# Cross-attention in another order: value projections spread over both pairs of heads, queries projected earlier, and the first batch's own work started on its own

## The chip, the core and the metric

The kernel runs on one core of a Trainium2 chip. The metric is the device time of one execution in microseconds (us). The engines are named as in the profile: PE is TensorE's matrix multiplication and PEld its weight loads, DVE is VectorE, ACT is ScalarE, POOL is GpSimd, SP is SyncE, which here only issues transfers.

## The reference, cut to what matters

Three layers follow one another on x of 4 batches x 256 tokens x 256. The change is in the first alone.

```
x = x + xattn(layernorm(x), ctx, Wq1, Wk1, Wv1, Wk2, Wv2, Wo, bo)   # the layer the change is in
x = x + mixer(layernorm(x), ...)                                    # top-k attention and a scan
x = x + experts(layernorm(x), ...)                                  # 8 experts, 2 of them per token

# xattn: 8 heads of 64, 256 queries, 256 own keys and 4096 context keys in each batch
q = x1 @ Wq1
k = concat(x1 @ Wk1, ctx @ Wk2)
v = concat(x1 @ Wv1, ctx @ Wv2)
attn = softmax(q @ k.T / 8)
return (attn @ v) @ Wo + bo
```

## The kernel before

`cross_attention` works through 16 pairs of heads, `u = 0..15`, four pairs for each of four batches. A pair has 4352 keys, in 17 tiles of 256 (`HG`), and is done in nine steps, `d = 0..8`; a step takes score tiles 2d and 2d+1, the last step only tile 16.

The projections keep single precision by splitting each operand in a high and a low part (`_hi`, `_lo`) and adding three products (`product3`, L609): ACT stores the high part, POOL or DVE subtracts to get the low part. For weights and context it is POOL that subtracts (L342, L347, L353).

While pair u is being scored and weighed, the same steps prepare pair v = u+1: `project_keys(v, d+1)`, 6 matmuls of 512 columns, and `score_for_max` (L677), two rough score products a step whose row maxima DVE reduces (L496). At the end of the pair `turn_maxima` (L688) turns the row maxima for the softmax shift, `store_neg_max` negates them on DVE, and only then can the next pair's `score` begin.

Values are projected for two pairs at a time (c = pair couple), 17 tiles of 12 matmuls each (`project_values`), in the PSUM banks M that `score_for_max` uses too. So a value tile waits until DVE has reduced the latest maxima (`max_reduced`), and the next `score_for_max` waits until ACT has stored the value tile (`v_stored`, L413). `v_due(u, d)` says which tiles belong to a step: before, two tiles in each of steps 2 to 8 of an odd pair, and the last three in steps 0 and 1 of the even pair after it.

The order on each engine is the order in which its function is written; engines meet only at semaphores. PE's order inside a step, before: maxima of the last key group, score tiles, maxima of this one, keys, values (L609), then the tiles of the step before weighed by the values (`weigh`, L722). At the end of a pair PE does the two last maxima products, three `weigh`, `turn_maxima`, then `project_queries(v)` and `project_keys(v, 0)` for the pair after.

DVE in a step: two maxima (L496), two additions of 128x1024 probabilities (L517), one low part of keys (L488). In step 1 it also inverts the sums and normalizes (L522, L531), which releases PE's first `weigh` of the pair.

At a change of batch the next batch's context chunks are loaded, copied and split in steps 3 and on of pair 4k+2 (`chunk_due`), and ACT and DVE split the own tokens (L459, L477) in its step 4. Before the first pair, all eight token tiles are normalized (DVE L104 to L123), turned by PE (L599) and copied (L472), and pair 0's keys, values and maxima are made; this is called the prologue here. Its first DVE instruction waits for x, bo and Wo together (`x_loaded`, 48).

## Time and profile before

| | us |
|---|---|
| median of three runs | 1687.1 (1685.04 to 1692.69) |
| the profiled execution | 1682.5 |
| its span in the trace | 1680.8 |
| prologue, to the first score of pair 0 | 79.7 |
| pairs 0 to 15, to the start of the mixer | about 1110 |
| PE busy over the whole span | 1475.6 (88%) |

The page's slices show PE at nine tenths or more almost all through the first 1180 us; only the first slice and the part after it are lower. Pair starts below are the start of the pair's first `score` matmul (L704). All numbers are of one profiled execution.

Four views are read below. A group of the page holds line, engine, operation and shapes, count, busy us and mean ns, and the idle time before it with its releaser. A row of the waits holds who waited for whom, total us, times and longest us. A row of busy times by stretch holds the stretch and its length in us, then the busy us (and instructions) of PE, PEld, DVE, ACT and POOL, then the clock granted to TensorE as a share of its full speed, the share of DMA time and GB/s. A row of the timeline holds start and duration in us, engine, line, operation, tiles, shape, how many alike were merged (x16) and, in brackets, how long the engine stood idle before it and who released it. The ends of matmuls are modelled, so distances between starts are used here for PE.

### The profile page before, as it was taken

To read this page: it belongs to the slowest core of one execution; us is meant where nothing else is said; L and a number is where in the kernel's file an instruction comes from. 1 tells how busy PE (TensorE), PEld (TensorE's weight loads), DVE (VectorE), ACT (ScalarE), POOL (GpSimd) and SP (SyncE) were. 2 spreads that over 40 slices of the span, in tenths; PEclk is the share of its full clock that TensorE was granted. 3 is DMA by queue.
4 is the path that set the end of the run, shared out by engine and by line. 5 is a ranking of instruction groups with operands and counts; after the bars stand their busy time and mean duration, and the time that the engine had idled before them with its cause. 6 is when DMAs were issued, how large, how long until landed. Compare 5 with 4: busy or idle time off the path is not lost. (4 is left out here: it accounts for less than half of the span.)

```text
span 1680.8 us, 29549 instructions
## 1 busy us (share of the span) xinstructions
PE 1475.6 (88%) x11988; PEld 1130.3 (67%) x11988; DVE 1128.8 (67%) x1287; ACT 711.3 (42%) x954; POOL 448.6 (27%) x270
## 2 busy tenths in 40 slices
PE   5999999999999999999999999999497787826996
PEld 4777776776776677677667777777264444526996
DVE  4587578557657855865876586486586899654663
ACT  3444344434434433343444344344336333223773
POOL 4300024000002400000230010000122999533885
PEclk9999999999999999999999999999799999967998
DMA  5000021000002100000210000000203900092333
GB/s 172 13 11 11 1 86 48 1 14 11 11 14 73 48 1 14 13 9 14 86 35 1 14 20 1 2 1 2 83 1 137 276 1 0 1 324 93 58 63 59
DMA packets 62371, 76.50 MB, mean 46 GB/s; under 512 B 6368, under 2 KB 47968, under 8 KB 61840
## 3 DMA queue, kind: packets, MB, share of 16 engines
q1 hardware_dynamic: 57152, 68.51, 13.3%
q0 software_dynamic: 5088, 6.11, 2.5%
q8 instruction: 99, 1.62, 0.4%
q14 instruction: 32, 0.26, 0.1%
HBM read 58.39 MB, written 17.25 MB: 45 GB/s over the span
## 5 line engine op out<-in xcount | busy, mean ns | idle before, releaser
L496 DVE TENSOR_REDUCE xa_maxes<-psum 128x2 f32<-128x1024 f32 (+1 forms) x288 | 332.5, 1161 | 268.9 <-PE psum L677 268.9
L422 ACT ACTIVATE xa_probs<-psum 128x1024 f32<-128x1024 f32 x272 | 269.1, 1026 | 325.4 <-PE psum L710 312.5
L517 DVE TENSOR_TENSOR xa_prob_sum<-xa_prob_sum,xa_probs 128x1024 f32<-128x1024 f32 x240 | 308.8, 1287 | 11.2 <-ACT xa_probs L422 10.4
L722 PE MATMUL psum<-xa_probs,xa_vals 128*64 128x256 f32 x2176 | 263.1, 385 | 2.2 <-DVE xa_heads_T L531 1.6
L722 PEld LDWEIGHTS psum<-xa_probs,xa_vals 128*64 128x64 f32 x2176 | 146.5, 136 | 92.7 <-issue 23.6
L347 POOL TENSOR_TENSOR xa_w_lo<-xa_stage,xa_w_hi 128x768 fp32r<-128x768 f32 x16 | 31.9, 1994 | 615.4 <-ACT xa_w_hi L382 615.4
L609 PE MATMUL psum<-xa_wv_hi,xa_ctx_hi 128*128 128x256 f32 x512 | 148.3, 290 | 21.2 <-DVE xa_maxes L496 18.4
L704 PE MATMUL psum<-xa_q_hi,xa_k_hi 64*128 64x256 f32 x1088 | 157.2, 285 | 0.6 <-issue 0.6
L708 PE MATMUL psum<-xa_q_hi,xa_k_lo 64*128 64x256 f32 x1088 | 155.1, 281 | 0.0
L710 PE MATMUL psum<-xa_neg_max,xa_ones 64*128 64x256 f32 x1088 | 154.7, 280 | 0.0
L706 PE MATMUL psum<-xa_q_lo,xa_k_hi 64*128 64x256 f32 x1088 | 154.5, 280 | 0.0
L413 ACT ACTIVATE xa_vals<-psum 128x512 f32<-128x512 f32 x136 | 81.2, 597 | 151.6 <-PE psum L609 151.6
L609 PE MATMUL psum<-xa_wv_lo,xa_ctx_hi 128*128 128x256 f32 x512 | 144.7, 283 | 0.0
L609 PE MATMUL psum<-xa_wv_hi,xa_ctx_lo 128*128 128x256 f32 x512 | 144.4, 282 | 0.0
L677 PE MATMUL psum<-xa_k_hi,xa_q_hi 64*128 64x512 f32 (+1 forms) x604 | 124.0, 425 | 16.8 <-issue 14.1
L404 ACT ACTIVATE xa_k_hi<-psum 128x512 fp32r<-128x512 f32 (+1 forms) x151 | 83.1, 555 | 129.6 <-PE psum L609 129.6
L609 PEld LDWEIGHTS psum<-xa_wv_hi,xa_ctx_hi 128*128 128x128 f32 x512 | 97.6, 191 | 41.3 <-issue 40.7
L488 DVE TENSOR_TENSOR xa_k_lo<-psum,xa_k_hi 128x512 fp32r<-128x512 f32 (+1 forms) x151 | 94.6, 630 | 37.9 <-ACT xa_k_hi L404 36.2
L609 PE MATMUL psum<-xa_ctx_hi,xa_w_hi 128*128 128x512 f32 x256 | 115.1, 450 | 2.5 <-issue 2.5
L1699 DVE TENSOR_TENSOR_SCAN mx_drive<-psum,mx_drive 128x768 f32<-128x768 f32 x64 | 110.0, 1743 | 7.7 <-POOL mx_drive L1224 6.9
L1224 POOL TENSOR_TENSOR mx_drive<-mx_xi,mx_rows 128x768 f32<-128x768 f32 x62 | 110.8, 1820 | 0.1
L342 POOL TENSOR_TENSOR xa_ctx_lo<-xa_ctx_in,xa_ctx_hi 128x1024 fp32r<-128x1024 f32 x32 | 84.8, 2652 | 93.8 <-ACT xa_ctx_hi L395 93.8
(319 smaller groups left out, 3013.1 us busy)
## 6 DMA issues: line engine op xcount, KB each, us to landing
xa_ctx_in<-in_ctxT_dram SPq DMA_DIRECT2D x32, 512.0 KB, 3.7
ex_slots<-mx_blank_tile SPq DMA_DIRECT2D x2, 4372.5 KB, 37.1
xa_stage<-in_L_xattn_Wk_dram SPq DMA_DIRECT2D x32, 128.0 KB, 2.4
xa_stage<-in_L_xattn_Wv_dram SPq DMA_DIRECT2D x16, 256.0 KB, 2.9
ex_raw<-in_L_ffn_w_gate_dram SPq DMA_DIRECT2D x8, 512.0 KB, 10.5
ex_raw<-in_L_ffn_w_up_dram SPq DMA_DIRECT2D x8, 512.0 KB, 10.9
ex_raw<-in_L_ffn_w_down_dram SPq DMA_DIRECT2D x8, 512.0 KB, 12.1
ex_xt<-ex_slots SPq DMA_DIRECT2D x15, 265.0 KB, 2.8
```

Of the source, the lines that this page charges most:

```text
L422: nc.scalar.activation(probs[:, n % RING, :], S[:, 2 * (n % 2):2 * (n % 2) + 2, :].rearrange("p h q -> p (h q)"), ACT.Exp, scale=HD ** -0. ...
L496: dve.tensor_reduce(maxes[:, qt, :, g:g + 1], max_banks(v, g, qt)[:, :, 0:group_keys(g)[1]], AX_X, ALU.max).then_inc(max_reduced, 1)
L517: dve.tensor_tensor(prob_sum[:, :], prob_sum[:, :], probs[:, n % RING, :], ALU.add).then_inc(summed, 1)
L609: i = pe.matmul(out, l, r, start=(c == 0 and k == 0), stop=(c == n - 1 and k == 2))
L677: i = pe.matmul(max_banks(v, g, qt)[:, h, part * N1:(part + slots) * N1], q_hi[half[h], v % 2, qt * P:(qt + 1) * P], k_hi[half[h], at:at + ...
L704: pe.matmul(out[h], k[h], q[h], start=True, stop=False)
L706: pe.matmul(out[h], k[h], q[2 + h], start=False, stop=False)
L708: pe.matmul(out[h], k[2 + h], q[h], start=False, stop=False)
L710: i = pe.matmul(out[h], ones[half[h], :], neg_max[half[h], :], start=False, stop=True)
L722: i = pe.matmul(O[half[h], 0:N1], vals[:, 2 * j + t, lanes:lanes + HD], probs[:, n % RING, (2 * h + t) * N1:(2 * h + t + 1) * N1], start=( ...
L1224: pool.tensor_tensor(drive[n % RINGS][:, :], dx[:, ct, :], b_rows[:, s, :], ALU.mult).then_inc(drive_done, 1)
L1699: dve.tensor_tensor_scan(drive[n % RINGS][:, :], decay[n % DECAYS], drive[n % RINGS][:, :], 0.0, ALU.mult, ALU.add).then_inc(scanned, 1)
```

## The change

It has four parts, all in `cross_attention`.

**Values.** `v_due` gives tiles 0 to 4 to steps 3 to 7 of the odd pair, 5 and 6 to its step 8, then 7 and 8, 9 and 10 to steps 0 and 1 of the even pair, and 11 to 16 to its steps 2 to 7. Within a step the value tile stands between the two `weigh`; in step 0 the sums of the pair before (`sum_probs`) go ahead of the values. In step 8 the maxima products are interleaved with the three `weigh`.

**Queries.** `project_queries(u + 2)` moves to the end of pair u, ahead of `turn_maxima`; for that the query and own-key weights are split apart from the context-key weights (`split_query_weights`, ACT and POOL, in step 6), and weights are loaded from step 0 on.

**Batches.** The own tokens stay as normalized rows (`xl_next`) and are turned by PE for one batch at a time (`turn_own`, 4 transposes, in step 0 of pair 4k+2), in the place of 16 transposes in the prologue. Context chunks are split four steps later: chunks 0 and 1 in steps 7 and 8 of pair 4k+2, chunks 2 to 7 in steps 0 to 5 of pair 4k+3.

**Start.** x is loaded in two parts. The first batch (`x_loaded`) is normalized and turned at once. The rest, bo and Wo are loaded between and behind the context chunks (`rest_loaded`, 48), and DVE waits for all three before it normalizes the other six tiles.

```diff
         def v_due(u, d):
             if u % 2 == 1 and u + 1 < U:
-                return [((u + 1) // 2, j) for j in (2 * d - 4, 2 * d - 3) if 0 <= j]
+                return [((u + 1) // 2, j) for j in ((5, 6) if d == STEPS - 1 else (d - 3,)) if j >= 0]
             if u % 2 == 0 and u > 0:
-                return [(u // 2, j) for j in (2 * d + 14, 2 * d + 15) if j < HG]
+                return [(u // 2, j) for j in ((7, 8) if d == 0 else (9, 10) if d == 1 else (9 + d,)) if j < HG]
             return []
...
-            at = (u % PAIRS - 2) * STEPS + d - 3
+            at = (u % PAIRS - 2) * STEPS + d - 7
...
-            sp.dma_start(X1[:, :, :], x.rearrange("b (t p) d -> p (b t) d", p=P)).then_inc(x_loaded, 16)
-            sp.dma_start(bo_sb, bo.rearrange("(a d) -> a d", a=1).broadcast_to([P, D])).then_inc(x_loaded, 16)
-            sp.dma_start(wo_sb[:, :, :], wo.rearrange("(c p) n -> p c n", p=P)).then_inc(x_loaded, 16)
+            sp.dma_start(X1[:, 0:QT, :], x[0, :, :].rearrange("(t p) d -> p t d", p=P)).then_inc(x_loaded, 16)
...
             load_pair(0)
-            for c in range(CHUNKS):
+            load_chunk(0, 0)
+            load_values(0)
+            load_chunk(0, 1)
+            sp.dma_start(X1[:, QT:TT, :], x[1:B, :, :].rearrange("b (t p) d -> p (b t) d", p=P)).then_inc(rest_loaded, 16)
+            sp.dma_start(bo_sb, bo.rearrange("(a d) -> a d", a=1).broadcast_to([P, D])).then_inc(rest_loaded, 16)
+            for c in range(2, CHUNKS):
                 load_chunk(0, c)
-                if c == 1:
-                    load_values(0)
+            sp.dma_start(wo_sb[:, :, :], wo.rearrange("(c p) n -> p c n", p=P)).then_inc(rest_loaded, 16)
             load_pair(1)
             for u, d in steps():
-                if d == 0 and u % 2 == 0 and u + 2 < U:
-                    load_values(u // 2 + 1)
-                if d == 4 and u % 2 == 0 and u + 2 < U:
-                    load_pair(u + 2)
-                if d == 0 and u % 2 == 1 and u + 2 < U:
+                if d == 0 and u % 2 == 1 and u + 1 < U:
+                    load_values((u + 1) // 2)
+                if d == 0 and u + 2 < U:
                     load_pair(u + 2)
...
@@ gpsimd, each pair @@
-                if d == 3 and u % 2 == 0 and u + 2 < U:
-                    split_values_weights(u // 2 + 1)
+                if d == 1 and u % 2 == 1 and u + 1 < U:
+                    split_values_weights((u + 1) // 2)
...
+                if d == 6 and u + 2 < U:
+                    split_query_weights(u + 2)
@@ vector @@
+            dve.wait_ge(x_loaded, 16)
+            norm.normalize(dve, 0, X1[:, 0:QT, :], xl_first)
             split_own(0)
             split_q(0)
             for g in range(NG):
                 split_keys(0, g)
+                if g == 1:
+                    dve.wait_ge(rest_loaded, 48)
+                    norm_rest.prepare(dve, 0, X1[:, QT:TT, :])
                 for qt in range(QT):
                     if g >= 1:
                         reduce_max(0, g - 1, qt)
+                if 2 <= g < 5:
+                    for t in (2 * g - 4, 2 * g - 3):
+                        norm_rest.apply(dve, 0, X1[:, QT:TT, :], xl_next, t)
...
@@ tensor, end of the prologue @@
+            project_keys(0, NG - 1, 0, 0)
+            for qt, j in enumerate(group_tiles(NG - 1)):
+                score_for_max(0, NG - 2, qt, 0)
+                project_values(0, j, 0)
+            score_for_max(0, NG - 1, 0, 0)
+            project_queries(1)
+            score_for_max(0, NG - 1, 1, 0)
             values = HG
             turn_maxima(0, values)
@@ tensor, each step @@
                 if following and d == 0:
-                    project_queries(v)
                     project_keys(v, 0, v * NG * QT, values)
+                    if own_due(u, d) is not None:
+                        turn_own(own_due(u, d))
...
+                    project_keys(v, d + 1, maxima, values)
+                    if d == 0 and u > 0:
+                        sum_probs(u - 1)
+                    for j in weighed[0:1]:
+                        weigh(u, j)
                     for c, j in v_due(u, d):
                         project_values(c, j, maxima)
                         values += 1
+                    for j in weighed[1:2]:
+                        weigh(u, j)
+                elif following:
+                    weigh(u, weighed[0])
+                    score_for_max(v, d, 0, values)
+                    weigh(u, weighed[1])
+                    score_for_max(v, d, 1, values)
                     weigh(u, HG - 1)
...
+                    if u + 2 < U:
+                        project_queries(u + 2)
+                    turn_maxima(v, values)
```

Places where the order of an engine changes. The line numbers are those of each kernel's own file; a row is an instruction, `x` is how many alike follow one another.

PE at the end of an even pair (pair 4, step 8), before. L677 are the maxima products, L722 the weighing, L688 `turn_maxima`, the rows behind it the queries:

```order
L710 MATMUL psum<-xa_neg_max,xa_ones 128x256 x2
L677 MATMUL psum<-xa_k_hi,xa_q_hi 128x512 x4
L722 MATMUL psum<-xa_probs,xa_vals 64x256 x12
L688 MATMUL psum<-ident,xa_max_cols 128x128 x2
L609 MATMUL psum<-xa_own_hi,xa_w_hi 128x256
```

The same place in the change (L741 maxima products, L786 weighing, L666 projections, L752 `turn_maxima`):

```order
L786 MATMUL psum<-xa_probs,xa_vals 64x256 x4
L741 MATMUL psum<-xa_k_hi,xa_q_hi 128x512 x2
L786 MATMUL psum<-xa_probs,xa_vals 64x256 x4
L741 MATMUL psum<-xa_k_hi,xa_q_hi 128x512 x2
L786 MATMUL psum<-xa_probs,xa_vals 64x256 x4
L666 MATMUL psum<-xa_own_hi,xa_w_hi 128x256
L666 MATMUL psum<-xa_own_lo,xa_w_hi 128x256
L666 MATMUL psum<-xa_own_hi,xa_w_lo 128x256
L666 MATMUL psum<-xa_own_hi,xa_w_hi 128x256
L666 MATMUL psum<-xa_own_lo,xa_w_hi 128x256
L666 MATMUL psum<-xa_own_hi,xa_w_lo 128x256
L752 MATMUL psum<-ident,xa_max_cols 128x128 x2
```

The two maxima products stand apart with a `weigh` before each, and the queries stand ahead of `turn_maxima`.

PE in step 7 of the same pair, before, from its last key product: no value tile, both `weigh` together.

```order
L609 MATMUL psum<-xa_ctx_lo,xa_w_hi 128x512
L609 MATMUL psum<-xa_ctx_hi,xa_w_lo 128x512
L722 MATMUL psum<-xa_probs,xa_vals 64x256 x8
L677 MATMUL psum<-xa_k_hi,xa_q_hi 128x512 x2
L704 MATMUL psum<-xa_q_hi,xa_k_hi 128x256 x2
```

And in the change, to the first of its value products:

```order
L666 MATMUL psum<-xa_ctx_lo,xa_w_hi 128x512
L666 MATMUL psum<-xa_ctx_hi,xa_w_lo 128x512
L786 MATMUL psum<-xa_probs,xa_vals 64x256 x4
L666 MATMUL psum<-xa_wv_hi,xa_ctx_hi 128x256
L666 MATMUL psum<-xa_wv_lo,xa_ctx_hi 128x256
```

The weighing is cut in two, and one value tile of 12 matmuls stands between the halves.

DVE in the prologue, before, from the low part of pair 0's queries (L488 low part of keys, L496 maxima):

```order
L482 TENSOR_TENSOR xa_q_lo<-psum,xa_q_hi 128x256
L488 TENSOR_TENSOR xa_k_lo<-psum,xa_k_hi 128x256
L488 TENSOR_TENSOR xa_k_lo<-psum,xa_k_hi 128x512
L496 TENSOR_REDUCE xa_maxes<-psum 128x2 x2
L488 TENSOR_TENSOR xa_k_lo<-psum,xa_k_hi 128x512
```

And in the change:

```order
L523 TENSOR_TENSOR xa_q_lo<-psum,xa_q_hi 128x256
L529 TENSOR_TENSOR xa_k_lo<-psum,xa_k_hi 128x256
L529 TENSOR_TENSOR xa_k_lo<-psum,xa_k_hi 128x512
L103 BN_STATS xa_norm_rest_stats<-X 128x6 x6
L106 BN_AGGR xa_norm_rest_agg<-xa_norm_rest_stats 128x2 x6
L108 TENSOR_SCALAR xa_norm_rest_var<-xa_norm_rest_agg 128x6
L110 RECIPROCAL xa_norm_rest_guess<-xa_norm_rest_root_var 128x6
L113 TENSOR_TENSOR xa_norm_rest_square<-xa_norm_rest_guess 128x6
L115 SCALAR_TENSOR_TENSOR xa_norm_rest_factor<-xa_norm_rest_square,xa_norm_rest_var 128x6
L118 SCALAR_TENSOR_TENSOR xa_norm_rest_rstd<-xa_norm_rest_factor,xa_norm_rest_guess 128x6
L537 TENSOR_REDUCE xa_maxes<-psum 128x2 x2
```

The statistics of the other six tiles, with the wait for `rest_loaded` ahead of them, stand before the first two maxima reductions.

## Rows read from the trace of the kernel before

**Rows 1.** Page, costly groups: count, busy us, mean ns, idle time before

```profile
L422 ACT ACTIVATE xa_probs<-psum 128x1024 f32<-128x1024 f32 x272 | 269.1, 1026 | 325.4 <-PE psum L710 312.5
L517 DVE TENSOR_TENSOR xa_prob_sum<-xa_prob_sum,xa_probs 128x1024 f32<-128x1024 f32 x240 | 308.8, 1287 | 11.2 <-ACT xa_probs L422 10.4
```

**Rows 2.** Busy time by stretch: pairs 5, 6 and 14

```profile
424.10:502.60 78.50, 76.02 (x691) 60.39 (x690) 46.87 (x51) 31.49 (x43) 1.81 (x1) 1.00 0.02 4
502.60:570.20 67.60, 60.83 (x555) 45.27 (x554) 53.79 (x51) 31.99 (x39) 20.96 (x8) 0.97 0.27 80
1082.90:1142.30 59.40, 57.10 (x542) 42.47 (x541) 45.66 (x49) 23.75 (x29) 0.00 (x0) 1.00 0.00 1
```

**Rows 3.** Waits of PE, 60 to 1190 us: total us, times, longest

```profile
PE psum L609 <- DVE xa_maxes L496: 21.8, 21, 1.4
PE psum L677 <- issue: 14.1, 19, 2.3
```

**Rows 4.** Timeline (start, us, engine, line), pair 8, step without values

```profile
698.08 0.50 PE L609 MATMUL psum<-xa_ctx_hi,xa_w_hi 128*128 128x512 f32 x1
...
699.67 1.95 PE L722 MATMUL psum<-xa_probs,xa_vals 128*64 128x256 f32 x16
701.54 0.50 PE L677 MATMUL psum<-xa_k_hi,xa_q_hi 64*128 64x512 f32 x2
...
704.10 0.50 PE L609 MATMUL psum<-xa_ctx_hi,xa_w_hi 128*128 128x512 f32 x1
```

**Rows 5.** Timeline, pair 7, step with two value tiles

```profile
603.94 0.50 PE L609 MATMUL psum<-xa_ctx_hi,xa_w_hi 128*128 128x512 f32 x1
...
605.67 0.35 PE L609 MATMUL psum<-xa_wv_hi,xa_ctx_hi 128*128 128x256 f32 x1
...
608.69 0.65 PE L722 MATMUL psum<-xa_probs,xa_vals 128*64 128x256 f32 x4
608.80 0.60 ACT L413 ACTIVATE xa_vals<-psum 128x512 f32<-128x512 f32 x1 [0.84 <-PE psum L609]
...
613.13 0.50 PE L609 MATMUL psum<-xa_ctx_hi,xa_w_hi 128*128 128x512 f32 x1
```

**Rows 6.** Timeline, step 8 of pairs 5 and 8

```profile
494.53 0.36 PE L609 MATMUL psum<-xa_wv_hi,xa_ctx_hi 128*128 128x256 f32 x1 [1.25 <-DVE xa_maxes L496]
...
709.45 0.73 PE L677 MATMUL psum<-xa_k_hi,xa_q_hi 64*128 64x512 f32 x4 [0.42 <-issue]
...
710.10 2.81 PE L722 MATMUL psum<-xa_probs,xa_vals 128*64 128x256 f32 x24
...
712.85 0.71 PE L688 MATMUL psum<-ident,xa_max_cols 128*128 128x128 f32 x4
```

**Rows 7.** Timeline, pair 6 step 1, PE's first value matmul

```profile
515.75 0.35 PE L609 MATMUL psum<-xa_wv_hi,xa_ctx_hi 128*128 128x256 f32 x1 [1.31 <-DVE xa_maxes L496]
```

**Rows 8.** Timeline, pair 6, which changes the batch

```profile
535.65 2.27 DVE L517 TENSOR_TENSOR xa_prob_sum<-xa_prob_sum,xa_probs 128x1024 f32<-128x1024 f32 x1
...
541.95 0.80 PE L677 MATMUL psum<-xa_k_hi,xa_q_hi 64*128 64x512 f32 x2 [2.24 <-issue]
...
568.07 0.39 PE L609 MATMUL psum<-xa_own_hi,xa_w_hi 128*128 128x256 f32 x1 [2.79 <-POOL xa_w_lo L347]
```

**Rows 9.** Start and prologue: timeline, then busy times by stretch

```profile
9.35 2.71 DVE L104 BATCH_NORM_STATS2 xa_norm_stats<-X 128x6 f32<-128x256 f32 x8 [9.35 <-DMA xa_wo<-in_L_xattn_Wo_dram]
...
14.65 2.67 DVE L123 TENSOR_SCALAR xa_xl<-X,xa_norm_agg,xa_norm_rstd 128x256 f32<-128x256 f32 x8
...
34.92 0.39 PE L677 MATMUL psum<-xa_k_hi,xa_q_hi 64*128 64x256 f32 x2 [0.88 <-DVE xa_maxes L496]
...
75.96 1.22 PE L688 MATMUL psum<-ident,xa_max_cols 128*128 128x128 f32 x4 [1.90 <-DVE xa_max_cols L501]
...
15.00:26.00 11.00, 6.17 (x27) 5.42 (x28) 8.64 (x19) 3.34 (x4) 7.61 (x3) 1.00 1.02 347
...
74.00:81.00 7.00, 5.11 (x30) 4.82 (x30) 3.14 (x6) 1.59 (x3) 0.00 (x0) 0.51 0.25 77
```

195 lines of the change are left out of this document (118 added, 77 removed).

## The prediction

> **What bounds the kernel now.** I read the page first, then the busy times by pair, then PE's waits, and last the timeline of single steps. The page puts the large groups on ACT and DVE, but with hundreds of us of idle time before them [rows 1]; inside a pair it is PE that is full, 76.0 of 78.5 us in pair 5 and 57.1 of 59.4 in pair 14, with DVE at 46.9 and 45.7 [rows 2]. The timeline tells what that means in a step. Without values, the first key matmul stands at 698.08, the weighing at 699.67, the next maxima at 701.54 and the next step's keys at 704.10 [rows 4]: 6.02 us from keys to keys, with no gap that a wait would explain. DVE has 45.7 us of work in the nine steps of pair 14 [rows 2], some 5.1 a step, so it is near but not the bound. A step with two value tiles takes 613.13 - 603.94 = 9.19 us [rows 5], and there too PE works through. So spreading values from steps that have two to steps that have none frees nothing by itself: **both kinds of step are bound by PE**, and the number of products stays the same. What can be won is only where PE waits. Between 60 and 1190 us its waits name 21.8 us for DVE's maxima (21 times) and 14.1 us ahead of the maxima products [rows 3], and 2.79 us at each of three changes of batch [rows 8]. That, some 44 us, and the start is all there is, and the change pays for what it takes.
>
> **Values between the weighings: a small loss in each step, a gain at its ends.** A cut weighing leaves PE's 64-column form once more. Two tiles weighed together take 701.54 - 699.67 = 1.87 us [rows 4], three take 712.85 - 710.10 = 2.75 [rows 6]; so one more tile costs 0.87 and each exit 0.14. Two value tiles with the entry to weighing take 608.69 - 605.67 = 3.02 [rows 5], one therefore 1.44 + 0.14 = 1.58. A step with one value tile is then 6.02 + 1.58 + 0.14 = 7.74, say 7.75 us, while half of 6.02 + 9.19 is 7.61. In the odd pair five steps go from 9.19 to 7.75 and one from about 9.3 (the first, with a longer wait) to 6.03, in the even pair six steps go from 6.03 to 7.75: -7.2 - 3.3 + 10.3 = -0.2 us for a couple of pairs. The switch from weighing to values stands nowhere in the trace. Its exit is between 0 (as from weighing to weighing) and 0.3; I take 0.14, that of rows 4 and 6, the same engine leaving the same form. The ends make 77 steps x 0.14 = 11 us either way.
>
> In step 8 PE now waits 0.42 us ahead of the maxima products, in all pairs, and 1.25 us ahead of the values in the odd ones [rows 6]. The interleaved weighings (0.87 each) cover both: the second maxima product comes one weighing after the first, and the weighing and the queries behind it (1.0 + 0.8 us) cover DVE's last two reductions of 1.2 us, which begin with the first product. Less two more exits and small differences: -0.1 in an even and -1.5 in an odd pair. In step 1 of the even pair the wait of 1.31 us for the maxima behind DVE's normalization [rows 7] is covered by the first weighing, but the step holds two value tiles in place of one (+1.44) and a cut (+0.14, and an entry): +0.4. In step 0 of the even pair `sum_probs` no longer stands behind the values. The next maxima product uses their banks and has to wait for ACT, which stores from 608.80 to 609.40 when the engine's next work could start at 608.69 [rows 5]: 0.7, +0.8 with the hand-over, a **new wait**. Together -0.2 - 1.6 + 0.4 + 0.8 = -0.6 for a couple, and up to 0.2 more by the small differences of the other steps, with 0.1 lost in step 1 of the odd pair, where POOL now splits the value weights beside DVE's inversion: some -0.7, seven couples, **-5 us** (-16 to +6 with the ends of the switch). In single-value steps the same store is covered: 0.8 against a weighing of 1.01, 0.2 us to spare. ACT is free for it, since its other work in the step, two exponentials of 1.03 [rows 1] and the keys' high part, ends before the value tile does.
>
> **Changes of batch.** Pair 6 takes 67.6 us [rows 2]; a plain even pair 60.2 (pair 14, 59.4, and 0.8 for the queries and keys that its last step lacks) [rows 2]. Pairs 2 and 10 are like pair 6 with 65.8, and the odd pairs behind the three exceed pair 5's 78.5 by 1.9, 1.5 and 1.9. The excess is 5.6 + 7.4 + 5.6 + 1.9 + 1.5 + 1.9 = 23.9 us. Two waits make most of it: 2.24 us at 541.95, when DVE was behind with the split of the own tokens, and 2.79 us at 568.07, when POOL had a chunk ahead of the weights that the queries needed [rows 8]. The change takes away both: the own tokens are split from PSUM in step 0 of the pair, and the query weights in step 6, before any chunk. What is late next is DVE: with a POOL split beside it an addition took 2.27 us [rows 8], where the mean is 1.29 [rows 1]. Chunks 2 to 7 now fall in steps 0 to 5 of the odd pair, and its step 1 also has the inversion, the normalization and the split of the value weights. I let one stretched addition in steps 0 to 2 (1.0) and half of a second reach PE: +1.6 us a batch. The four transposes of `turn_own` with their entry are 1.0 at most. So -23.9 + 3 x 1.6 + 3 x 1.0 = **-16 us** (-21 if no stretch shows, -11 if three additions reach PE).
>
> The Trainium skill, page SBUF — State Buffer, section "Who interferes with whom", has the port that DVE and GpSimd share as an exclusive lock, in which the later one waits out the whole instruction. The trace agrees in kind, with 2.27 us for an addition of 1.29; an addition that waits out a split would lose more than that 1.0, and by it the batches would lose up to 4 us more.
>
> **End of the prologue.** PE waits 1.90 us ahead of `turn_maxima` at 75.96, after shorter waits for maxima, and from 74 to 81 us the granted clock is 0.51 of full speed, the lower of TensorE's two levels (1.2 GHz) [rows 9]. The new order puts two value tiles and the queries between the maxima. DVE's last reduction stays to be waited for, so `turn_maxima` comes some 1.0 us earlier. Behind it stand 6 matmuls of 256 columns in place of 12 (3.7 us from 75.96 to the first score at 79.7): 1.4 us, or 2.2 at the low clock. -1.0 - 2.3 = **-3.3 us** (-1 to -5).
>
> **Start.** The first query matmul stands at 23.7 now; it could stand near 10, with only a quarter of x awaited. But DVE, after the low part of key group 1, waits for `rest_loaded`, that is for Wo behind all context chunks, and the first maxima reduction stands behind it. The value weights are issued once POOL has split the weights, near 9 us (x lands near 4, normalization of two tiles some 3, transposes, own split), and their first packets move 1.4 us later. From there 5504 KB (value weights 512, chunks 3584, x 768, bo 128, Wo 512), 5.64 MB, must land at 347 GB/s [rows 9]: 16.2 us, so near 27. The statistics then take 4.4 us (14.65 - 9.35 = 5.3 for eight tiles, less two tiles' share of 0.4 each [rows 9]), the first reduction 0.7: PE's second maxima product at 32.3 in place of 34.92 [rows 9], -2.6. By then PE has stood idle some 9 us, and after the shorter waits ahead of 76 us the granted clock was low for 7 us [rows 9]; as long a stretch here costs 3.4. **+0.8 us** (-10 if the transfers are early, +4).
>
> **Sum.** -5 - 16 - 3.3 + 0.8 = -23.5 us. Nothing behind the cross-attention changes. Against the profiled execution (1682.5, span 1680.8) that is 1659; this execution lies 4.6 below the median of the runs, 1687.1, so 1663.
>
> **Rivals.** (a) *The start keeps its lead.* x's rest and Wo land before 20 us, or PE passes on before it needs the reduction: 10 us instead of 0, 1653. Against it stand the bytes and the 347 GB/s; for it only that I built the time of issue from several links. 15%. (b) *Leaving a form drains PE.* The change adds 77 cuts. If each of the two new switches costs what one exit costs by rows 4 and 6 and as much again, a step pays 0.32 in place of 0.14, 77 x 0.18 = 14 us more: 1677. Rows 4 and 6 speak against it, with 0.14 for one exit. The Trainium skill, page TensorEngine Tiling (Array Packing), section "Key Properties", says that a change of tiling mode drains the engine, and gives no price; the trace agrees that it costs something. 12%. (c) *The value store is not out in time*, so the end is **slower than before**. It decides in every single-value step: if ACT's store (0.60) comes more than 0.2 us later than I have it, the next maxima product waits. If ACT reaches it one instruction late, 0.6 us, PE loses 0.4 to 0.6 in each of 77 steps, 31 to 46 us: 1694 to 1709, 1700. ACT's 31.5 us of work in the 78.5 of pair 5 [rows 2] speak against it. 5%. (d) *DVE falls behind for good at the changes of batch and in the odd steps 1*, which eats the 16 us and 3 more: 1682. 8%. That the change doesn't do what it says can be left out: the rows of order show values and queries at their new places.
>
> **How the numbers follow.** The forecast, 1663, has 60%. Around it the switch (11 us either way) and the batches (5) make 1652 to 1674, and the cases (a) and (b) lie at its ends; the range takes in both and runs from 1648 to 1680, and leaves out (c), most of (d) and a lucky sum of lows. A measurement of this kernel can tell 0.5%, 8.4 us, from no change. Faster by more than that (under 1678.7): all of the forecast, (a) and most of (b), 87%; within: (d), the rest of (b), 8%; slower: (c), 5%.
>
> **What the profile will show.** Single-value steps 7.75 us apart, by the first key matmul; over 7.9 means (b), over 8.1 with PE waiting at the maxima products (c). Step 8: no wait ahead of the maxima. Even step 0: PE waits 0.8 us for ACT's values. Pairs 2, 6 and 10 within 2 us of their neighbours without an output projection. In the start: DVE idle until Wo lands, near 27, and PE idle from about 23 to 32; if DVE starts its second set of statistics before 20, the start is mis-sized and (a) holds. Should the single-value steps stand under 7.6 us, PE was not the bound in the steps without values, and my first step is wrong.

## The result, and the profile after

The changed kernel takes 1670.5 us (median of four runs, 1668.14 to 1671.36), the kernel before, run beside it, 1686.07 (1684.53 to 1692.69). The ratio is 0.9899 (95% interval 0.9878 to 0.992): 15.6 us faster by the medians. 1663.0 was forecast, with 1648 to 1680 as its range. The profiled execution of after took 1671.36 us with a span of 1669.4. Of the four executions of run 3 below, one took 3814.42 us and is left out of that run's ratio; without it its median is 1659.44 in place of 1659.83.

Busy times of pairs 5, 6 and 14, the columns as in [rows 2]:

```profile
417.30:484.90 67.60, 67.23 (x611) 49.92 (x610) 48.82 (x52) 28.72 (x39) 5.24 (x4) 1.00 0.05 15
1053.50:1125.30 71.80, 69.92 (x627) 51.85 (x626) 45.59 (x48) 27.90 (x36) 0.14 (x1) 1.00 0.00 1
484.90:556.90 72.00, 71.22 (x639) 53.28 (x638) 45.79 (x48) 31.23 (x41) 6.35 (x4) 1.00 0.22 65
```

Pair 5 now takes 67.6 us where it took 78.5, pair 14 takes 71.8 where it took 59.4: value tiles have moved from odd to even pairs, and the sum of a couple has hardly moved. (The 67.6 hold 0.9 for `turn_own`, which stands ahead of pair 6's first score.) Pair 6, which changes the batch, takes 72.0, like any even pair. PE is busy for 71.2 of these; before it was 60.8 of 67.6.

PE's waits from 60 to 1190 us, as in [rows 3], without one of a later stage:

```profile
PE psum L741 <- ACT xa_vals L458: 5.5, 7, 0.8
PE psum L666 <- DVE xa_maxes L537: 3.3, 9, 0.4
...
PE psum L741 <- issue: 2.0, 4, 1.0
```

The 21.8 us for DVE's maxima (21 times) are now 3.3, and the 14.1 us ahead of the maxima products are 2.0. A new row has come in: 5.5 us, in seven pieces of up to 0.8, for ACT's store of values. The mean addition on DVE has not become shorter:

```profile
L558 DVE TENSOR_TENSOR xa_prob_sum<-xa_prob_sum,xa_probs 128x1024 f32<-128x1024 f32 x240 | 312.8, 1303 | 11.3 <-ACT xa_probs L467 10.4
```

A step with one value tile, pair 5 (first starts, from keys to the next keys; compare [rows 4] and [rows 5]):

```profile
444.88 0.51 PE L666 MATMUL psum<-xa_ctx_hi,xa_w_hi 128*128 128x512 f32 x1
...
446.48 1.08 PE L786 MATMUL psum<-xa_probs,xa_vals 128*64 128x256 f32 x8
447.49 0.38 PE L666 MATMUL psum<-xa_wv_hi,xa_ctx_hi 128*128 128x256 f32 x1
...
449.11 1.08 PE L786 MATMUL psum<-xa_probs,xa_vals 128*64 128x256 f32 x8
450.13 0.50 PE L741 MATMUL psum<-xa_k_hi,xa_q_hi 64*128 64x512 f32 x2
...
452.68 0.51 PE L666 MATMUL psum<-xa_ctx_hi,xa_w_hi 128*128 128x512 f32 x1
```

From 444.88 to 452.68 it is 7.80 us, with no wait: DVE's reduction, which the values need, ended 1.1 us before they start. Keys take 1.60, the first weighing 1.01, the values 1.62, the second weighing 1.02.

Step 0 of pair 6, ACT's last value store and the maxima product behind it, and then step 8 of the same pair (compare [rows 6]):

```profile
492.88 0.60 ACT L458 ACTIVATE xa_vals<-psum 128x512 f32<-128x512 f32 x1 [0.84 <-PE psum L666]
```

```profile
493.62 0.39 PE L741 MATMUL psum<-xa_k_hi,xa_q_hi 64*128 64x256 f32 x2 [0.78 <-ACT xa_vals L458]
...
551.93 0.51 PE L741 MATMUL psum<-xa_k_hi,xa_q_hi 64*128 64x512 f32 x2
...
553.38 0.50 PE L741 MATMUL psum<-xa_k_hi,xa_q_hi 64*128 64x512 f32 x2
```

The first is the new wait, 0.78 us. In step 8 neither maxima product has a wait in brackets.

Pair 3, a change of batch, step 4. POOL splits a context chunk, DVE adds and then reduces, and PE's value tile waits for the reduction:

```profile
298.40 1.23 DVE L537 TENSOR_REDUCE xa_maxes<-psum 128x2 f32<-128x1024 f32 x1 [1.85 <-PE psum L741]
298.57 2.41 POOL L361 TENSOR_TENSOR xa_ctx_lo<-xa_ctx_in,xa_ctx_hi 128x1024 fp32r<-128x1024 f32 x1 [5.97 <-ACT xa_ctx_hi L440]
...
299.54 2.52 DVE L558 TENSOR_TENSOR xa_prob_sum<-xa_prob_sum,xa_probs 128x1024 f32<-128x1024 f32 x1
301.98 1.21 DVE L537 TENSOR_REDUCE xa_maxes<-psum 128x2 f32<-128x1024 f32 x1
```

```profile
303.45 0.36 PE L666 MATMUL psum<-xa_wv_hi,xa_ctx_hi 128*128 128x256 f32 x1 [0.36 <-DVE xa_maxes L537]
```

The start, timeline and then busy times by stretch (compare [rows 9]):

```profile
29.54 2.06 DVE L103 BATCH_NORM_STATS2 xa_norm_rest_stats<-X 128x6 f32<-128x256 f32 x6 [5.54 <-DMA xa_wo<-in_L_xattn_Wo_dram]
...
34.23 0.58 PE L741 MATMUL psum<-xa_k_hi,xa_q_hi 64*128 64x256 f32 x2 [9.32 <-DVE xa_maxes L537]
```

```profile
24.90:28.10 3.20, 0.00 (x1) 0.00 (x0) 0.00 (x0) 0.33 (x1) 2.17 (x1) 1.00 1.05 325
28.10:34.20 6.10, 0.00 (x0) 0.01 (x1) 4.03 (x18) 0.21 (x1) 0.00 (x0) 0.50 0.06 16
34.20:38.30 4.10, 4.08 (x12) 3.29 (x13) 0.69 (x1) 0.60 (x2) 0.00 (x0) 0.50 0.02 4
...
74.00:81.00 7.00, 5.45 (x56) 4.61 (x55) 3.89 (x7) 3.59 (x6) 5.56 (x9) 1.00 0.22 59
```

DVE waits for Wo until 29.5, and PE stands still from 24.9 to 34.2. The granted clock is at the lower level (0.50, 1.2 GHz) for the second part of that and for 4.1 us of work behind it. The stretch from 74 to 81, which ran at 0.51 before, runs at 1.00 in this trace.

**Where the time went**, by the starts of the pairs in the two traces (changed minus before, us):

| place | forecast | measured |
|---|---|---|
| start, to the second keys behind the maxima product of [rows 9] (40.34, now 41.47) | +0.8 | +1.1 |
| end of the prologue (pair 0 starts at 78.0 in place of 79.7) | -3.3 | -2.8 |
| pair 0 | (in the last two rows) | -0.5 |
| three changes of batch | -16 | -16.1 |
| seven couples of pairs, the rest | -5 | +1.3 |
| sum: start of pair 15, 1142.3 to 1125.3 | -23.5 | -17.0 |

The measured rows for batches and couples are split with a plain couple, 138.7 before (pairs 5 and 14, and the 0.8 of the prediction) and 138.8 after (66.8 + 72.0). Nearly the whole shortfall of 6.5 us is in the couples. The rows differ in how sure they are. From the start of pair 1 to that of pair 15 a kernel repeats within 0.1 us from trace to trace (before 1007.7 and 1007.8; with the changed kernel's pairs 992.9, 993.0 and 992.9). The start of pair 0 does not: with the changed kernel's prologue it is 78.0 here and 76.5 to 79.5 in runs 3 to 7. So the first three rows carry 1 to 2 us either way.

### The profile page after: what moved, and what is told of

Same layout as the page of the kernel before. It is cut to its first block and busy times, and to the rows that moved or that the text cites. A ratio compares the mean times of both kernels' runs of the same rounds, so it can differ in the third digit from the quotient of the medians.

```text
span 1669.4 us, 29627 instructions
## 1 busy us (share of the span) xinstructions
PE 1499.5 (90%) x11988; PEld 1117.0 (67%) x11988; DVE 1124.1 (67%) x1283; ACT 712.0 (43%) x971; POOL 451.4 (27%) x286
## 3 DMA queue, kind: packets, MB, share of 16 engines
q8 instruction: 99, 1.62, 0.4%
## 5 line engine op out<-in xcount | busy, mean ns | idle before, releaser
L558 DVE TENSOR_TENSOR xa_prob_sum<-xa_prob_sum,xa_probs 128x1024 f32<-128x1024 f32 x240 | 312.8, 1303 | 11.3 <-ACT xa_probs L467 10.4
L786 PE MATMUL psum<-xa_probs,xa_vals 128*64 128x256 f32 x2176 | 288.2, 390 | 2.1 <-DVE xa_heads_T L572 1.5
L786 PEld LDWEIGHTS psum<-xa_probs,xa_vals 128*64 128x64 f32 x2176 | 136.2, 136 | 104.6 <-issue 42.1
L367 POOL TENSOR_TENSOR xa_w_lo<-xa_stage,xa_w_hi 128x512 fp32r<-128x512 f32 x16 | 20.7, 1291 | 565.8 <-ACT xa_w_hi L414 565.8
L666 PE MATMUL psum<-xa_wv_hi,xa_ctx_hi 128*128 128x256 f32 x512 | 154.3, 301 | 3.4 <-DVE xa_maxes L537 3.3
L666 PE MATMUL psum<-xa_wv_lo,xa_ctx_hi 128*128 128x256 f32 x512 | 144.6, 282 | 0.0
L666 PE MATMUL psum<-xa_wv_hi,xa_ctx_lo 128*128 128x256 f32 x512 | 144.3, 282 | 0.0
L741 PE MATMUL psum<-xa_k_hi,xa_q_hi 64*128 64x512 f32 (+1 forms) x604 | 128.3, 431 | 16.8 <-DVE xa_maxes L537 9.3
L666 PEld LDWEIGHTS psum<-xa_wv_hi,xa_ctx_hi 128*128 128x128 f32 x512 | 97.4, 190 | 39.8 <-issue 39.4
L666 PE MATMUL psum<-xa_ctx_hi,xa_w_hi 128*128 128x512 f32 x256 | 115.4, 451 | 2.5 <-issue 2.5
```

Of the source, the lines that this page charges most:

```text
L558: dve.tensor_tensor(prob_sum[:, :], prob_sum[:, :], probs[:, n % RING, :], ALU.add).then_inc(summed, 1)
L666: i = pe.matmul(out, l, r, start=(c == 0 and k == 0), stop=(c == n - 1 and k == 2))
L741: i = pe.matmul(max_banks(v, g, qt)[:, h, part * N1:(part + slots) * N1], q_hi[half[h], v % 2, qt * P:(qt + 1) * P], k_hi[half[h], at:at + ...
L786: i = pe.matmul(O[half[h], 0:N1], vals[:, 2 * j + t, lanes:lanes + HD], probs[:, n % RING, (2 * h + t) * N1:(2 * h + t + 1) * N1], start=( ...
```

## The experiments

All edits are to the changed kernel unless said otherwise. Times are medians; the kernel before, beside these runs, had 1687.5 to 1688.0, some 1.6 us more than beside the changed kernel's own, so 1670.5 stands here as about 1672. Where a few us matter I go by the starts in the traces.

**1. Wo apart.**

```
-            ...wo...).then_inc(rest_loaded, 16)
+            ...wo...).then_inc(wo_loaded, 16)       # POOL waits for it, ahead of the bias
...
-                    dve.wait_ge(rest_loaded, 48)
+                    dve.wait_ge(rest_loaded, 32)
```

> Wo gets a semaphore of its own, and DVE waits in front of its second statistics only for the rest of x and for bo, which stand ahead of six context chunks in the queue. Theory 1 (the start gives its lead away at the wait for Wo, 29.5 us in the changed kernel, and PE's idle time there also costs the full clock): the statistics start near 20, PE's idle stretch of 9.5 us falls to 2 or 3 us, the granted clock stays at 1.0 or is low for a shorter time, and pair 0 starts 7 to 10 us earlier, 1661 to 1663 by the median. Rival (the context chunks bound the prologue anyway, Wo or not): pair 0 starts within 2 us of the changed kernel's 78.0, 1669 to 1671.

Measured: 1663.8, ratio 0.9858 (0.983 to 0.9886). Pair 0 starts at 74.4 in place of 78.0, ahead of all six traces with the old place of the wait (76.5 to 79.5). The gain is half of what I had written down, because the wait for Wo was not all that stood there:

```profile
23.38 0.69 DVE L531 TENSOR_TENSOR xa_k_lo<-psum,xa_k_hi 128x512 fp32r<-128x512 f32 x1 [4.57 <-ACT xa_k_hi L451]
...
23.99 2.05 DVE L103 BATCH_NORM_STATS2 xa_norm_rest_stats<-X 128x6 f32<-128x256 f32 x6
...
29.08 0.58 PE L743 MATMUL psum<-xa_k_hi,xa_q_hi 64*128 64x256 f32 x2 [4.01 <-DVE xa_maxes L539]
```

The statistics begin at 24.0, at once behind the keys' low part, for which DVE had idled 4.57 us. PE still waits 4.0 us for the reduction behind them.

**2. The statistics early as well.** Run 1, and:

```
-                if g == 1:
+                if g == 0:
                     dve.wait_ge(rest_loaded, 32)
                     norm_rest.prepare(dve, 0, X1[:, QT:TT, :])
...
-                if g == 1:
+                if g == 0:
                     norm_rest.root(act, 0)
```

> As the run with Wo apart, and the second statistics stand behind key group 0 on DVE and ACT, in place of group 1, where DVE stood idle for 4.6 us. Theory 1 (the start is bound by DVE's place in line for x's rest, not by the transfers of the context): PE's wait of 4.0 us ahead of the second maxima product falls under 1 us, pair 0 starts near 70.5 in place of 74.4, total near 1660. Rival (the rest of x lands after 21, or PE then waits for chunk 1 or the keys' split instead): pair 0 at 73 to 75, total 1662 to 1665.

Measured: 1662.05, ratio 0.9844 (0.9819 to 0.9868). Pair 0 starts at 69.4, better than the 70.5 expected, though PE's wait is 2.4 us and not under 1:

```profile
20.12 2.06 DVE L103 BATCH_NORM_STATS2 xa_norm_rest_stats<-X 128x6 f32<-128x256 f32 x6 [2.22 <-DMA xa_heads_T<-in_L_xattn_bo_dram]
...
27.51 0.38 PE L743 MATMUL psum<-xa_k_hi,xa_q_hi 64*128 64x256 f32 x2 [2.37 <-DVE xa_maxes L539]
```

Theory 1 holds: 8.6 us of the start's lost lead come back by the place of two waits, with the same bytes in the same order. Runs 9 and 10, with the same start, have pair 0 at 70.2 and 69.3. From 20 to 40 us the granted clock is 1.00 all through. By the medians the step from run 1 is only 1.8 us; behind pair 15 this profiled execution took 538 us and run 1's 535 (see run 11).

**3. Two value tiles in a step again**, in the new order.

```
-  ... for j in ((5, 6) if d == STEPS - 1 else (d - 3,)) if j >= 0]
+  ... for j in (2 * d - 4, 2 * d - 3) if 0 <= j]
-  ... for j in ((7, 8) if d == 0 else (9, 10) if d == 1 else (9 + d,)) if j < HG]
+  ... for j in (2 * d + 14, 2 * d + 15) if j < HG]
```

> The value tiles go back to two in a step (odd pair steps 2 to 8, even pair steps 0 and 1), in the new order of a step, with one weighing ahead of them and one behind. Theory 1 (both kinds of step are bound by PE, so spreading is worth nothing but the cuts): two-value steps 9.3, steps without values 6.03, a couple of pairs within 1 us of 138.8, total within 5 us of 1670.5. Rival (spreading relieves DVE or ACT in the steps that had two tiles or none): a couple 2 us longer or more, total 1684 or more.

Measured: 1659.8, ratio 0.9824 (0.9784 to 0.9864), some 12 us **faster** than the changed kernel. Neither theory had this sign at this size. Pair 15 starts at 1114.8 in place of 1125.3. A step with two tiles:

```profile
447.57 0.51 PE L666 MATMUL psum<-xa_ctx_hi,xa_w_hi 128*128 128x512 f32 x1
...
450.19 0.38 PE L666 MATMUL psum<-xa_wv_hi,xa_ctx_hi 128*128 128x256 f32 x1
...
456.81 0.51 PE L666 MATMUL psum<-xa_ctx_hi,xa_w_hi 128*128 128x512 f32 x1
```

9.24 us. Two tiles add 9.24 - 6.02 = 3.22 to a step without values, one adds 7.80 - 6.02 = 1.78. The second tile of a block (value tiles that follow one another) thus costs 1.44, and having a block between the weighings 0.34, whatever it holds. A couple of pairs has 9 such blocks with two in a step (7 steps of the odd pair, 2 of the even) and 14 when spread (6 and 8): 5 x 0.34 = 1.7 us a couple. Pairs 5 and 6 show it, 139.6 against 78.1 + 59.8 = 137.9. Seven couples make 12 us: from pair 1 to pair 15 it takes 980.9 us in place of 992.9. Pair 15 has 10.5 of that, since pair 1 started 1.5 later in this trace.

**4. The values ahead of both weighings**, one tile in a step.

```
-                    for j in weighed[0:1]:
-                        weigh(u, j)
                     for c, j in v_due(u, d):
                         project_values(c, j, maxima)
                         values += 1
-                    for j in weighed[1:2]:
+                    for j in weighed:
                         weigh(u, j)
```

> The cut in the weighing is undone: one value tile in a step as in the changed kernel, but ahead of both weighings instead of between them (steps 0 to 7; step 8 unchanged). Theory 1 (a cut costs one more exit from the 64-column form, 0.14 us, in 70 or so steps): single-value steps 7.66 in place of 7.80, total 1660 to 1662. Rival A (the weighing between keys and values covers the reduction of the maxima, which the values' bank waits for, so the cut pays for itself): the values wait for DVE by 0.14 us or more, steps 7.80 to 8.0, total 1670 to 1685. Rival B (the values' switch drains far more than 0.14): steps 7.5 or less, total under 1655.

Measured: 1671.9, ratio 0.9914 (0.9886 to 0.9941). From pair 1 to pair 15 it takes 995.1 us, 2.2 more than the changed kernel.

```profile
444.45 0.50 PE L666 MATMUL psum<-xa_ctx_hi,xa_w_hi 128*128 128x512 f32 x1
...
444.71 1.22 DVE L537 TENSOR_REDUCE xa_maxes<-psum 128x2 f32<-128x1024 f32 x1
...
445.71 0.40 PE L666 MATMUL psum<-xa_ctx_hi,xa_w_lo 128*128 128x512 f32 x1
...
446.19 0.36 PE L666 MATMUL psum<-xa_wv_hi,xa_ctx_hi 128*128 128x256 f32 x1
...
452.22 0.50 PE L666 MATMUL psum<-xa_ctx_hi,xa_w_hi 128*128 128x512 f32 x1
```

The step is 7.77 us, only 0.03 less than with the cut. But this is not the price of the cut, because PE waits in this order. The reduction ends at 444.71 + 1.22 = 445.93 and the values start 0.26 us behind it; in the ordinary steps of this run it is 0.25 to 0.29 each time. From the last key product to the first value product it is 446.19 - 445.71 = 0.48, where key products stand 0.23 apart. The brackets don't show the wait, since PE's modelled ends cover it.

Step 2 of pairs 4, 8 and 12 has the same order without the wait, because the output projection stands between the maxima product and the keys there, and the reduction is done 4.5 us ahead of the values. In this run:

```profile
365.72 0.47 PE L666 MATMUL psum<-xa_ctx_hi,xa_w_hi 128*128 128x512 f32 x1 [0.83 <-issue]
...
366.95 0.39 PE L666 MATMUL psum<-xa_ctx_hi,xa_w_lo 128*128 128x512 f32 x1
367.18 0.28 PE L666 MATMUL psum<-xa_wv_hi,xa_ctx_hi 128*128 128x256 f32 x1
...
373.15 0.50 PE L666 MATMUL psum<-xa_ctx_hi,xa_w_hi 128*128 128x512 f32 x1
```

And in the changed kernel:

```profile
365.71 0.47 PE L666 MATMUL psum<-xa_ctx_hi,xa_w_hi 128*128 128x512 f32 x1 [0.83 <-issue]
...
373.47 0.51 PE L666 MATMUL psum<-xa_ctx_hi,xa_w_hi 128*128 128x512 f32 x1
```

It is 7.43 us without the cut and 7.76 with it, and 5.99 in run 3, which has no values in that step; pairs 8 and 12 agree within 0.03. So a value tile right behind the keys costs 7.43 - 5.99 = 1.44, no more than a second tile does: the block costs nothing. **The cut costs 0.33**, and in ordinary steps it saves a wait of 0.3. Rival A (the cut pays for itself) has the mechanism right in every single-value step. It shows most where DVE is later: without the cut step 1 of the even pairs takes 9.69 in place of 9.26, and step 3 behind a change of batch 9.1 in place of 8.4, with 10.5 us of waits for DVE's maxima in place of 3.3.

**5. Each value tile in two halves**, one ahead of the first weighing and one behind it.

```
+                    due = v_due(u, d)
+                    apart = len(due) == 1 and d >= 2
+                    if apart:
+                        project_values(*due[0], maxima, (0,))
                     for j in weighed[0:1]:
                         weigh(u, j)
-                    for c, j in v_due(u, d):
-                        project_values(c, j, maxima)
+                    for c, j in due:
+                        project_values(c, j, maxima, (1,) if apart else (0, 1))
```

> The changed kernel, with the single value tile of a step in two halves of six matmuls each, one half ahead of the first weighing and one behind it, so that each of 77 steps has one more block of value matmuls and no more products. Theory 1 (a block of values costs 0.30 us for entering and leaving it, however long it is, which is why two tiles in one block were cheaper): single-value steps 8.10 in place of 7.80, 77 x 0.30 = 23 us more than 1670.5, near 1693. Rival (only the cut of the weighing costs, 0.04 us by the run with the values ahead; the rest is a wait for DVE or ACT in single-value steps): steps 7.80 to 7.90, total 1670 to 1678.

Measured: 1704.1, ratio 1.011 (1.008 to 1.0141).

```profile
457.74 0.51 PE L666 MATMUL psum<-xa_ctx_hi,xa_w_hi 128*128 128x512 f32 x1
...
459.49 0.36 PE L666 MATMUL psum<-xa_wv_hi,xa_ctx_hi 128*128 128x256 f32 x1
...
461.38 0.39 PE L666 MATMUL psum<-xa_wv_hi,xa_ctx_hi 128*128 128x256 f32 x1
...
465.86 0.51 PE L666 MATMUL psum<-xa_ctx_hi,xa_w_hi 128*128 128x512 f32 x1
```

8.12 us by these rows, 8.10 by most steps: 0.30 more for one more block with the same 12 matmuls, as theory 1 had it. But the cause is the one that the rival names. The first half stands right behind the keys, and in ordinary steps it waits for DVE's reduction as in run 4 (it starts 0.26 us behind the reduction's end). Step 2 of pair 4, where nothing is awaited:

```profile
376.74 0.47 PE L666 MATMUL psum<-xa_ctx_hi,xa_w_hi 128*128 128x512 f32 x1 [0.83 <-issue]
...
384.50 0.51 PE L666 MATMUL psum<-xa_ctx_hi,xa_w_hi 128*128 128x512 f32 x1
```

7.76 us (7.75 and 7.74 in pairs 8 and 12), the same as the changed kernel. One more block without one more cut costs nothing. The total is 11 us over the 1693 expected, since the first half has no weighing ahead of it: in steps 3 to 6 of pairs 3, 7 and 11 it waits for the delayed reduction, and those steps take 9.4 us.

The Trainium skill, page TensorEngine Tiling (Array Packing), section "Key Properties", says that a change of tiling mode drains the engine. The runs agree that such changes cost something: keys and values have the same form (128*128 in the rows), a weighing another (128*64), so a cut brings two changes more, for 0.33 us, and run 5's block brings none, for nothing. That a drain is what takes the time, no run shows.

**6. The sums behind the values** in step 0 of the even pairs.

```
-                    if d == 0 and u > 0:
-                        sum_probs(u - 1)
                     for j in weighed[0:1]:
                         weigh(u, j)
                     for c, j in v_due(u, d):
                         project_values(c, j, maxima)
                         values += 1
+                    if d == 0 and u > 0:
+                        sum_probs(u - 1)
```

> In step 0 of the even pairs the four sum matmuls of the pair before stand behind the two value tiles again, as in the kernel before, in place of ahead of them. Theory 1 (the wait for ACT's store of the second tile, 0.8 us in each of 7 even pairs, goes under them, and the later sums are covered in step 1): step 0 of an even pair 8.1 in place of 8.9, total 5 us less, 1665. Rival (DVE's inversion and normalization now begin 2.9 us later, and step 1's weighing or maxima wait for them): step 1 longer by what step 0 gains, total within 1.5 us of 1670.5.

Measured: 1665.4, ratio 0.9873 (0.9843 to 0.9904). Step 0 falls from 8.93 to 7.9, step 1 rises from 9.26 to 9.69: 0.6 us a couple, 4 in all, between the two expectations. The new wait is gone, the row has no brackets:

```profile
493.59 0.39 PE L741 MATMUL psum<-xa_k_hi,xa_q_hi 64*128 64x256 f32 x2
```

**7. The chunks split four steps earlier**, `d - 3` in place of `d - 7` in `chunk_due`.

> One number of the changed kernel: the eight context chunks of the next batch are split four steps earlier (from step 3 of pairs 2, 6 and 10 on, as in the kernel before, in place of step 7). Six of them then fall in single-value steps of 7.80 us and two, in place of three, in steps without values of 6.02. Theory 1 (what is left at a change of batch is DVE's additions stretched by POOL's splits beside them, which reach PE in steps 3 to 6 of pairs 3, 7 and 11 with 8.2 to 8.4 us): those steps return to 7.80 and pairs 2, 6, 10 stay at 72.0, total 5 us less, 1665. Rival (the stretch only moves: the same loss in pairs 2, 6 and 10, or the query weights wait behind a chunk on POOL): the couple of the change of batch at 140.6 or more, total 1669 to 1675.

Measured: 1668.8, ratio 0.9897 (0.9868 to 0.9926). The rival holds: steps 4 to 7 of pairs 2, 6 and 10 now take 8.2 in place of 7.80, steps 4 to 6 of pairs 3, 7 and 11 are back at 7.80. From pair 1 to pair 15 it takes 994.1 us in place of 992.9: four steps a batch lose 0.4 where three did. (Pair 15 starts at 1125.0, 0.3 early, only because pair 0 started 1.5 early in this trace; the medians can't tell a difference of 1.2.) The loss of 0.4 us goes with the split, into whichever step holds both a split and values. Steps without values (6.02 in both) show none of it themselves.

**8. In the kernel before, the weights ahead of the chunk.** In step 8 ACT and POOL do `split_weights(u + 2)` before `split_chunk`, in place of after it.

> The kernel before, with one thing changed: in step 8 ACT and POOL split the pair weights ahead of the context chunk, in place of behind it. Theory 1 (of the 24 us that the changes of batch cost before, the three waits of 2.8 us are POOL's chunk ahead of the query weights): those three waits go, pairs 2, 6 and 10 are 2.4 to 2.8 us shorter, total 7 to 8 us less than the kernel before. Rival (the weights are late because of their load, or the later chunk split makes keys or values wait in the next pair): pairs 3, 7 and 11 longer by what 2, 6 and 10 gain, total within 2 us of the kernel before.

Measured: 1672.1, ratio 0.9921 (0.9894 to 0.9947).

```profile
558.08 1.83 POOL L347 TENSOR_TENSOR xa_w_lo<-xa_stage,xa_w_hi 128x768 fp32r<-128x768 f32 x1 [1.17 <-ACT xa_w_hi L382]
559.86 3.38 POOL L342 TENSOR_TENSOR xa_ctx_lo<-xa_ctx_in,xa_ctx_hi 128x1024 fp32r<-128x1024 f32 x1
```

The weights are ready at 559.9 and the query product stands at 560.42 without a wait. Step 8 of pairs 2, 6 and 10 falls from 10.1, 10.6 and 10.1 to 7.0, a little more than the waits of 2.8, and pair 15 starts at 1132.6 in place of 1142.3, 9.7 us earlier. So of the 16 us of the changes of batch more than half come from two swapped calls. The medians differ by 15.3; where the other 5.6 us of the runs that were not profiled lie stays open. In the kernel before, the granted clock stood at 0.50 for 3.4 us behind each of the three waits (from 278.9, 569.0 and 859.1 us); in run 8 it is 1.00 at these places.

**9. Runs 2, 3 and 6 together.**

> Wo apart, the second statistics early, two value tiles in a step and the sums behind the values, all together in the changed kernel. Theory 1 (the four act in different places: start, value blocks, even step 0): 10 + 10.7 + 4 us less than the changed kernel, near 1646; odd two-value steps 9.24, steps without values 6.03, even step 0 7.9. Rival (sums late in an even step 1 that holds one tile has no cover: DVE's normalization is awaited there): even step 1 over 8.3 in place of 7.82, total 1650 or more.

Measured: 1646.9, ratio 0.9756 (0.9725 to 0.9787). The steps are as theory 1 has them (9.24, 6.03, even step 0 at 7.9), and even step 1 is 8.25, under the 8.3 of the rival but over 7.82. Pair 15 starts at 1103.2, 22.1 us before that of the changed kernel.

**10. And DVE's reduction ahead of the addition** where POOL is splitting.

```
+                late = 3 <= d < STEPS - 1 and chunk_due(u, d - 1) is not None
-                if d >= 2 and not (d == STEPS - 1 and v < U):
+                if d >= 2 and not late and not (d == STEPS - 1 and v < U):
                     add_probs(u, 2 * d - 1)
                 if v < U:
                     reduce_max(v, d, 0)
+                if late:
+                    add_probs(u, 2 * d - 1)
```

> As the run with all four edits together, and in the steps in which POOL splits a context chunk (steps 3 to 6 of pairs 3, 7 and 11) DVE takes the reduction of the maxima ahead of the addition of the probabilities. Theory 1 (the addition is what POOL's split holds up, 2.5 us in place of 1.2, and the reduction that the values' bank waits for only stands behind it): those steps fall from 9.64 to 9.24, 12 x 0.41 = 5 us less, near 1642. Rival (the delay only moves to the split of the keys behind it, or the reduction from PSUM is held up as well): the steps stay at 9.5 to 9.7 or the next score waits for DVE, total 1646 to 1648.

Measured: 1642.0 (1638.99 to 1644.57), ratio 0.9743 (0.971 to 0.9776). The twelve steps fall from 9.64 to 9.24, and the row of waits for DVE's maxima, 4.4 us in run 9, is gone. The reductions, which read PSUM, run at full speed beside POOL's split (560.90 to 563.31), and both additions start behind it:

```profile
560.73 1.23 DVE L539 TENSOR_REDUCE xa_maxes<-psum 128x2 f32<-128x1024 f32 x1 [2.28 <-PE psum L746]
562.84 1.23 DVE L539 TENSOR_REDUCE xa_maxes<-psum 128x2 f32<-128x1024 f32 x1 [0.89 <-PE psum L746]
563.99 2.54 DVE L560 TENSOR_TENSOR xa_prob_sum<-xa_prob_sum,xa_probs 128x1024 f32<-128x1024 f32 x2
```

This is the fastest of all versions here, 2.6% under the kernel before.

**11. The kernel before, once more.**

> The kernel before, unchanged, for a second trace of it. Theory 1 (the 4.6 us between its profiled execution and the median of its runs lie in the stages behind the cross-attention, whose stretches at the lower clock fall differently): pair 15 starts within 2 us of 1142.3. Rival (the gap is in the changes of batch, where PE's waits of 2.8 us bring the lower clock in some executions): pair 15 starts 3 us or more off 1142.3, in pairs 2 to 12.

Measured: 1688.3. Pair 15 starts at 1141.8, 0.5 off the first trace, and the rest takes 539.0 us (to the store of the output at 1680.8) where it took 532.8 (1142.3 to 1675.1). Theory 1 holds: the gap of 4.6 us between the profiled execution of before and its median lies behind the cross-attention, in stages that the change does not touch. Adding it to the sum was right, as far as two traces tell.

## Why the prediction was right, and where it was not

**PE as the bound: right but for one wait that I missed.** In run 3 and in the changed kernel the values of ordinary steps start some 1.1 us behind DVE's reduction, with nothing to wait for. In the kernel before they did wait, in the ordinary steps with two value tiles. To [rows 5] belongs this row of DVE:

```profile
604.19 1.22 DVE L496 TENSOR_REDUCE xa_maxes<-psum 128x2 f32<-128x1024 f32 x1
```

It ends at 605.41 and the values start at 605.67, the same 0.26 us behind it as in run 4. In step 0 of the even pairs, where it ends 0.7 us before, they follow the keys without a gap. So the 9.2 us of such a step are 6.02 + 2 x 1.44 + 0.3 of waiting, and "there too PE works through" was wrong. There are 34 such steps, some 10 us, which were not among the 44 us of waits that I took for all there was. The change removes these waits by its cuts and pays 0.33 for each cut, so it is about even there.

**Single-value step: 7.75 forecast, 7.80 measured, out of two errors that nearly cancel.** I had 0.14 for the cut, and it costs 0.33. I had 0.14 for leaving the block, and the block costs nothing: where nothing is awaited the values start 1.50 us behind the keys (step 0 of pair 6), sooner than a weighing (1.59 [rows 4]), and that makes up for their exit. The 1.73 from keys to values in [rows 5] showed the wait, and I never compared it with the 1.59. So 6.02 + 1.58 + 0.14 came out well by luck.

**"Spreading frees nothing": right, but it is not free either.** This is the step of the prediction that failed in kind, though its own sum for the couple (-0.2, measured +0.2) hid it. I weighed the new order and the spreading as one. Run 3 separates them: the order and the rest of the change are worth some 28 us (1687.8 to 1659.8), and spreading gives 12 of them back, by five more cuts in each couple.

**Couples: -5 forecast, +1.3 measured, the whole of the shortfall.** By steps of a plain couple: values +0.2 (forecast -0.2), odd step 8 less its part of `turn_own` -1.4 (-1.5), even step 8 0.0 (-0.1), even step 0 +1.0 (+0.8), even step 1 +0.15 (+0.4), and odd step 0 +0.17, 5.04 to 5.21, which I did not have. The sum is +0.1 where -0.7 stood. None of these terms is off by more than 0.4, but they count seven times.

**The new wait for ACT's store: right** in place, count and size (0.8, 7 times, 5.5 us), and run 6 shows that order alone makes it; the 0.6 us that it wins back in a couple are less than 0.8, since the cover in step 1 costs part of it.

**Changes of batch: -16 forecast, -16.1 measured.** Run 8 confirms the second of the two waits, POOL's chunk ahead of the weights, at its price or a little more (3.1 to 3.6 us off the step in place of 2.8). The loss that I put in their place, stretched additions, is there with 1.8 us a batch (1.6 forecast), but in steps 3 to 6 and not 0 to 2. In steps 4 to 6 it is the values that wait for the reduction, 0.4 each; in step 3 it is a maxima product behind a late reduction, 0.6, which stays in run 7, where a split stands beside the same addition. `turn_own` costs 0.9 (at most 1.0 forecast), which stands at the ends of pairs 1, 5 and 9. Runs 7 and 10 show the mechanism. The Trainium skill, page SBUF — State Buffer, section "Who interferes with whom", has DVE and GpSimd share a port as an exclusive lock. The trace agrees, with the addition waiting out the whole split: the one that starts at 299.54 ends at 302.06, 1.08 us behind the end of POOL's split at 300.98 (alone it takes 1.22). In either kernel there are 15 additions that start beside a chunk's split, and all of them end 1.08 or 1.09 us behind its end. The 2.27 us of [rows 8], which I took for the size of the loss, is one of them; it is shorter because it started later beside its split.

**End of the prologue: -3.3 forecast, -2.8 measured.** `turn_maxima` comes at 76.61, behind a start that is 1.1 later, and the lower clock doesn't fall there in this trace. In runs 3, 5 and 6, with the same prologue, it does (in stretches from 75.9 to 82.8 us), and pair 0 starts at 78.5, 78.9 and 79.5; without it, in runs 4 and 7, at 76.8 and 76.5. So the forecast's size can't be told from the spread.

**Start: +0.8 forecast, +1.1 measured,** again out of two errors. Wo landed later than I had it (statistics at 29.5, not 27), so PE's second maxima product came at 34.2 and was 0.7 ahead of the old place, not 2.6. The lower clock cost less: from there to the second keys it is 41.47 - 34.23 = 7.2 us where it was 40.34 - 34.92 = 5.4, so 1.8 in place of 3.4, since most of the low stretch fell in idle time. Rival (a) did not come, since DVE waited as said; runs 1 and 2 show that its 8.6 us were to be had.

**Rivals (b), (c), (d).** (c) did not occur: no maxima product waits in a single-value step, and the margin of 0.2 us held. (d) is there at 1.8 us a batch and no more. (b) has the cut's price right, 0.33 us measured where it had 0.32. The single-value steps stayed under its 7.9 because the 0.14 that the sum had for the block was not there.

## What to carry to other kernels

When work is spread over more steps, count the changes of form as well as the products: on an engine that is full, each place that brings two more of them has a fixed price, here 0.33 us. A short wait need not show as idle time. It shows when the start of a product keeps the same distance to the end of what it needs (here 0.26 us) while its distance to the product ahead is longer than usual (0.48 in place of 0.23). Compare it with the same place where nothing is awaited before giving the time to something else. Test each half of a combined change by itself, since a good half can pay for a bad one without showing it. And look at what stands in front of a wait in program order: two swapped calls, an own semaphore for one load and a reduction put ahead of an addition gave 9.7, 8.6 (with the statistics moved) and 5 us here, each without changing any work.
